# A graph network on one core: who gathers the rows of 782 steps, and how many of them are gathered ahead

## The reference

```python
# round 0
e = relu((x[dst] - x[src]) @ theta_w.T + theta_b + x[src] @ phi_w.T + phi_b)
x = layernorm(x + segment_max(e, dst))            # 0 where a node has no edge
# rounds 1 and 2
hv = x @ W_in + b_in
for W, b in ((W_u0, b_u0), (W_u1, b_u1)):
    m = relu(concat([hv[src], he]) @ W + b)       # he: 64 features of each edge
    hv = where(has_in, segment_max(m, dst) + hv, hv)
x = layernorm(x + relu(hv @ W_ro + b_ro))
```

## Time and profile before

| | |
|---|---|
| median of 3 runs | 4331.12 us (4325.9 to 4362.31) |
| span of the profiled execution, first to last instruction | 3216.1 us |
| time of the profiled execution | not given; the median is 1115.0 us over the span |
| busy: TensorE, GpSimd, VectorE, ScalarE | 2494.2, 2359.0, 1457.3, 196.1 us |
| mean granted TensorE clock | 0.922 |
| moved by DMA | 762.66 MB, mean 237 GB/s |
| gathers of steps: from x, from tables | 34, 2288 |
| row fetches of SyncE | 3072 |

### The profile page before, as it was taken

One profiled execution on the slowest core, in us unless ns is written; L12 is line 12 of the kernel. 1 busy time (PEld: TensorE's weight loads), 2 busy tenths in 40 slices (PEclk: granted clock), 3 DMA queues, 4 the chain that ended last, 5 costly groups with the idle time before them and its releaser, 6 DMA issues.

```text
span 3216.1 us, 33579 instructions
## 1 busy us (share of the span) xinstructions
PE 2494.2 (78%) x6386; PEld 1183.3 (37%) x6386; DVE 1457.3 (45%) x3424; ACT 196.1 (6%) x439; POOL 2359.0 (73%) x2484
## 2 busy tenths in 40 slices
PE   8776666666676888887887888688888888888877
PEld 6432222222223533333333333353333344333335
DVE  2675556555556533333433334323333343333337
ACT  2000000000002400000000000010000000000005
POOL 5777777777776677777777777667777777777765
PEclk9898888788877999999999999899999999999989
DMA  7666667666665777777777777687777777777764
GB/s 263 232 223 222 225 224 268 221 224 214 211 210 191 246 242 244 245 244 244 245 252 246 245 244 247 207 271 249 250 251 252 252 267 247 253 249 252 250 210 153
DMA packets 266593, 762.66 MB, mean 237 GB/s; under 512 B 57652, under 2 KB 113823, under 8 KB 229903
## 3 DMA queue, kind: packets, MB, share of 16 engines
q0 software_dynamic: 118896, 324.63, 33.2%
q1 hardware_dynamic: 94110, 356.95, 28.8%
q10 hardware_dynamic: 53376, 78.93, 7.9%
HBM read 413.88 MB, written 346.41 MB: 236 GB/s over the span
## 4 chain that ended last, share of the span: by engine, by line
POOL 39%; PE 17%; DMA 16%; issue 16%; SPq 7%; DVE 2%; ACT 2%; DVEq 0%; ACTq 0%; POOLq 0%
POOL gath L606 38%; DMA gath<-table,src_sb 14%; PE edge_ps L887 6%; SPq L530 4%; PE edge_ps L885 3%; PE edge_ps L778 3%; SPq L526 2%; PE side_ps L778 2%; PE edge_ps L864 2%; POOL gath L633 1%; DVE hist L410 1%; ACT x_sb L718 1%; DMA runs<-hist 1%; SPq L529 1%; DMA table<-hist 1%
## 5 line engine op out<-in xcount | busy, mean ns | idle before, releaser
L606 POOL DMA_INDIRECT gath<-table,src_sb x2288 | 2165.4, 946 | 745.0 <-issue 649.6
L410 DVE SCALAR_TENSOR_TENSOR hist<-hist,lift,edge_ps 128x256 f32<-128x256 f32 x2346 | 1127.0, 480 | 1564.3 <-PE edge_ps L887 1142.8
L887 PE MATMUL edge_ps<-gath,ident 128*128 128x512 f32 x1548 | 842.6, 627 | 328.0 <-DMA gath<-table,src_sb 326.4
L885 PE MATMUL edge_ps<-w_e,he_sb 128*128 128x512 f32 x1564 | 813.9, 602 | 5.5 <-DMA he_sb<-in_he 5.0
L864 PE MATMUL edge_ps<-gath,ident 128*128 128x512 f32 x740 | 476.3, 767 | 269.9 <-DMA gath<-table,src_sb 164.2
L887 PEld LDWEIGHTS edge_ps<-gath,ident 128*128 128x128 f32 x1548 | 275.7, 193 | 803.9 <-DMA gath<-table,src_sb 595.9
L885 PEld LDWEIGHTS edge_ps<-w_e,he_sb 128*128 128x128 f32 x1564 | 295.4, 194 | 352.7 <-issue 335.0
L864 PEld LDWEIGHTS edge_ps<-gath,ident 128*128 128x128 f32 x740 | 155.5, 236 | 532.5 <-DVE hist L410 317.1
L676 ACT COPY hv_sb<-side_ps 128x256 f32<-128x256 f32 x147 | 54.8, 373 | 2770.2 <-PE edge_ps L887 1842.9
L633 POOL DMA_INDIRECT gath<-runs,end_row x147 | 152.1, 1035 | 49.0 <-issue 43.6
L786 PE MATMUL edge_ps<-dst_f,onehot 128*128 128x512 f32 x200 | 78.0, 514 | 14.2 <-DVE onehot L333 14.2
(11 more groups left out here) (137 smaller groups left out, 1070.6 us busy)
## 6 DMA issues: line engine op xcount, KB each, us to landing
runs<-hist SPq DMA_DIRECT2D x285, 1024.0 KB, 5.0
he_sb<-in_he ACTq DMA_DIRECT2D x194, 256.0 KB, 2.9
late_sb<-table SPq DMA_DIRECT2D x3072, 1.0 KB
gath<-table,src_sb POOLq DMA_INDIRECT x2288, 3.4
table<-hist SPq DMA_DIRECT2D x72, 256.0 KB, 3.4
back_T<-x1T ACTq DMA_DIRECT2D x98, 128.0 KB, 3.2
runs<-hist SPq DMA_DIRECT2D x33, 256.0 KB, 2.9
x_sb<-in_x SPq DMA_DIRECT2D x49, 128.0 KB, 2.8
```

The source lines that it names most:

```text
L410: state = V.scalar_tensor_tensor(hist[:, s % H, :], hist[:, (s - 1) % H, :], lift[:, t:t + 1], edges, ALU.add, ALU.max)
L606: pool.indirect_dma_start(gath[:, s % G, :], None, a["x"] if s < RAW else tables[r], bass.IndirectOffsetOnAxis(src_sb[:, t:t + 1], 0)).the ...
L885: T.matmul(bank, he_sb[:, c % NHE, at:at + P], w_e[r - 1][:, :], start=True, stop=False)
L887: last = T.matmul(bank, ident[:, :], flat(edge_rows(s)), start=False, stop=True)
```

## The change

The two blocks of steps that SyncE fetched row by row go back to GpSimd, and all of `late_rows` goes, with its buffer `late_sb` (4 steps). The ring grows from 34 to 38 slots. Round 0's first 50 steps are gathered from x: 38 into the ring and 12 (`SPILL`) into tiles 32 to 43 of `x_sb`, which holds no features until later. `ring_place` leaves those 12 out of the ring's count, so step 50 takes the slot of step 0, step 88 that of step 50, and from there on a step waits for the step 38 before it. All 50 are raw for TensorE and ScalarE: 25 pairs are turned, copied and multiplied, where 17 were.

```diff
-G, H = 34, 24
+G, H = 38, 24
-RAW = G
-LATE_AT = (360, 720)
-LATE = 4
-LATE_ROWS = 16
+SPILL, SPILL_TILE = 12, 32
+RAW = G + SPILL
...
+        spill = x_sb[:, SPILL_TILE:SPILL_TILE + SPILL, :]
...
-        def by_pool(t):
-            return t < STEPS and late_group(t) is None
+        def real(t):
+            return t < STEPS
+
+        def in_spill(s):
+            return G <= s < RAW
+
+        def ring_place(s):
+            return s if s < G else s - SPILL
...
             def store_runs(r):
                 for c in range(CHUNKS):
-                    late_rows(r, c)
...
             def gather_edges(r):
-                for t in filter(by_pool, range(STEPS)):
+                for t in range(STEPS):
                     s = r * STRIDE + t
-                    if s % GS == 0 and s >= G:
-                        pool.wait_ge(group_summed, groups_to(s - G))
+                    if s % GS == 0 and s >= RAW:
+                        before = ring_place(s) - G
+                        pool.wait_ge(group_summed, groups_to(before if before < G else before + SPILL))
...
-                    pool.indirect_dma_start(gath[:, s % G, :], None, a["x"] if s < RAW else tables[r],
-                                            bass.IndirectOffsetOnAxis(src_sb[:, t:t + 1], 0)
-                                            ).then_inc(gathered[s % G // 2], 16)
+                    if in_spill(s):
+                        pool.indirect_dma_start(spill[:, s - G, :], None, a["x"],
+                                                bass.IndirectOffsetOnAxis(src_sb[:, t:t + 1], 0)
+                                                ).then_inc(spilled[(s - G) // 2], 16)
+                    else:
+                        pool.indirect_dma_start(gath[:, ring_place(s) % G, :], None, a["x"] if s < RAW else tables[r],
+                                                bass.IndirectOffsetOnAxis(src_sb[:, t:t + 1], 0)
+                                                ).then_inc(slot_filled(s), 16)
...
             def turn_raw(n):
-                pe.wait_ge(gathered[n], 2 * 16)
+                if in_spill(2 * n):
+                    pe.wait_ge(spilled[n - G // 2], 2 * 16)
+                else:
+                    pe.wait_ge(gathered[n], 2 * 16)
```

More of the change, by code:

```diff
@@ L37 @@
 XT_FIRST, XT_UNITS = 4, 3
-RAW = G
-LATE_AT = (360, 720)
-LATE = 4
-LATE_ROWS = 16
+SPILL, SPILL_TILE = 12, 32
+RAW = G + SPILL
 CONV, NEXT0, NEXT1, OUT = range(4)
-LATE_TURN = 3
-WEIGHTS_AT = (LATE_TURN + 1) * BODY
+EARLY_TURNS = 3
+WEIGHTS_AT = (EARLY_TURNS + 1) * BODY
 FIRST_X_CHUNK = 20
+assert SPILL % GS == 0 and SPILL_TILE + SPILL <= TILES
 assert TURNS == TILES and STRIDE % SC == 0 and H % SC == 0 and G % GS == 0 and STRIDE % HC == 0 and HC % GS == 0 and SC % GS == 0
@@ L174, in gnn_kernel @@
         raw_out = sem("raw_out")
+        spilled = [sem(f"spilled{q}") for q in range(SPILL // 2)]
         staged_written = [sem(f"staged_written{b}") for b in range(UNIT_BUFS)]
@@ L221, in groups_to, with slot_filled @@
             return s // STRIDE * GROUPS + min(s % STRIDE // GS + 1, GROUPS)
-        def late_group(t):
-            return next((n for n, first in enumerate(LATE_AT) if first <= t < first + LATE), None)
-        def by_pool(t):
-            return t < STEPS and late_group(t) is None
-        def pairs_in_slot(s):
-            return sum(by_pool(2 * q % STRIDE) for q in range(s // 2 % (G // 2), s // 2 + 1, G // 2))
+        def real(t):
[4 more added lines that the diff above has]
+            return s if s < G else s - SPILL
+        def pairs_in_slot(s):
+            at = ring_place(s) // 2
+            steps = [2 * q if 2 * q < G else 2 * q + SPILL for q in range(at % (G // 2), at + 1, G // 2)]
+            return sum(real(step % STRIDE) for step in steps)
+        def slot_filled(s):
+            return gathered[ring_place(s) % G // 2]
         def edge_rows(s):
[L233 to L236, removed]
+            if in_spill(s):
+                return spill[:, s - G:s - G + 2, :]
+            at = ring_place(s) % G
+            return gath[:, at:at + 2, :]
         def uses(n, u):
@@ L277, in back_tiles @@
         def back_tiles(r, i):
-            if r == 0 and i < 2 * (LATE_TURN + 2):
-                return range(max(0, 2 * (i - LATE_TURN - 2)), max(0, 2 * (i - LATE_TURN - 1)))
+            if r == 0 and i < 2 * (EARLY_TURNS + 2):
+                return range(max(0, 2 * (i - EARLY_TURNS - 2)), max(0, 2 * (i - EARLY_TURNS - 1)))
             return range(i, i + 1)
@@ L558, in write_out @@
                     sp.dma_start(a["out"][lo * P:NODES, :], outs(u)[0:left, 0, :]).then_inc(out_written[u % UNIT_BUFS], 16)
-            for n, first in enumerate(LATE_AT):
-                with nc.allow_non_contiguous_dma("small layouts"):
-                    sp.dma_start(late_src[n:n + 1, :].rearrange("o (p k) -> (o p) k", k=LATE), a["src"][:, first:first + LATE]
-                                 ).then_inc(late_listed, 16)
             for u in range(NU):
@@ L843, in wait_rows @@
             def wait_rows(s):
[L844 to L849 removed]
+                pe.wait_ge(slot_filled(s), 2 * 16 * pairs_in_slot(s))
             def first_rows():
@@ L870, in first_rows @@
                             back(t)
-                    if turn_no == LATE_TURN and at == BODY // 2 + GS:
+                    if turn_no == EARLY_TURNS and at == BODY // 2 + GS:
                         multiply_weights()
```

35 lines of the change are left out of this document (3 added, 32 removed).

## The result

The changed kernel took 3810.3 us, the median of 4 runs (3801.0 to 3815.8). The kernel before took 4346.7 us beside it (4 runs, 4325.9 to 4383.5). The ratio is 0.8785, with a 95% interval from 0.8735 to 0.8835: 12% less, where 0.9% more was forecast. The executions of this study ran on several chips. On two later ones the same pair stands at 3254.7 us against 3217.8, ratio 1.0115 (1.0100 to 1.0131), and at 3261.8 against 3226.3. I call the chips on which before takes 4334 us or more kind A (numbers 13 and 15, and the unnumbered chip of this result), and those on which it takes 3218 to 3226 us kind B (12 and 7). They differ in every kernel that ran on both. The runs come in series; within one series all kernels ran on one chip, and ratios are taken there only.

What follows compares the result with a forecast made beforehand. GpSimd's gathers, 1.25 us from start to start, were taken to set each round's end. 30.0 us for more gathers plus 8.8 at the start, added to 4331.1, gave 4369.9 us (+0.9%), range 4342 to 4393.

Steps and rivals of the forecast that it cites:

- part 1: GpSimd gathers 24 more steps over three rounds at 1.25 us each, +30.0 us; SyncE's dropped fetches are worth nothing.
- I take what lies around the span as unchanged: Outside the profiled span: the 1115.0 us between span and median time stay, so 38.8 us are added to 4331.1.
- signs of being wrong: TensorE sums step 68 before 158, the 1.25 us pace bends, a round's tail changes, or time minus span isn't 1115.
- Faster: Rival: SyncE's fetches cost time outside the span; if it went by number of instructions, 216 us, giving 4154; chance 0.07.
- rival of the stretched kernel: Rival: timed executions are the profiled one stretched by 1.347, so the change costs +52 us, giving 4383; chance 0.18.
- Sum: Whole kernel: 30.0 for the gathers plus 8.8 for the start gives +38.8 us, a span of 3254.9.
- Part 3: Round 0's start: TensorE's eight more raw pairs at 2.17 us make GpSimd wait 6.6 us at step 88, to 121.6.
- Part 4: ScalarE's weight loads queue behind raw copies; weight products come 12.3 us later, GpSimd is 8.8 us late from step 106.
- Part 2: Round 0's start: 16 more steps gathered from x in GpSimd's gap win 18.6 us, before TensorE's lag is counted.

Runs made afterwards that it cites:

- f3_half_dense: Kernel before with GpSimd gathering all steps and SyncE's fetches unused, but only half of them, batches of 16 in half as many chunks: 4063.2 us.
- f4_half_thin: Kernel before with GpSimd gathering all steps and SyncE's fetches unused, but only half of them, batches of 8 in as many chunks: 3827.0 us.
- h2_no_fetch_again: Kernel before without SyncE's fetches, GpSimd gathering all steps, ring of 34 and old start, on kind B: 3250.8 us, 1.0103 of before.
- h3_skip24: Kernel before with 24 steps neither fetched nor gathered, other rows summed in their place, on kind B: 3218.7 us, 1.0003 of before.
- h1_after_again: The changed kernel, nothing further altered, run again on kind B: 3254.7 us, 1.0115 of the kernel before.
- g1_incs_only: Kernel before without fetches, all steps gathered, plus 48 idle semaphore increments on SyncE in each of 192 chunks, on kind A: 3968.0 us, 0.915 of before.
- f1_static_rows: Kernel before with all steps gathered and SyncE's 3072 fetches unused, their row numbers written in the code, no register loads: 3816.1 us.
- f2_loads: Kernel before with all steps gathered and SyncE's fetches unused, all register loads kept but one fetch per batch of sixteen: 3784.9 us.

## Why the prediction was wrong

The step that failed is in part 1, on SyncE's 3072 fetches: their leaving "is worth nothing by itself: SyncE is on no chain that ends a round". On kind A, where the times were taken, the fetches are worth 628 us, 14% of the kernel, and SyncE is 40% of the chain. The premise was wrong in the profile of before, too: SyncE's queue has 7% of that chain, from 171.58 to 485.92. And the price of 0.23 us is a fetch's own duration; from one to the next it is 0.41, and with the load a batch fills nine tenths of a chunk. The forecast also took that one profile for the executions that had been timed. With it failed the line "I take what lies around the span as unchanged". On kind A the kernel before has a span of 4421.1 us in 4422.9, so the 1115 us lay inside the executions, in waits that the profile of before doesn't contain. Two of the prediction's own signs of being wrong came on kind A: the pace of 1.25 us bends, and the difference of time and span is not 1115.

The Trainium skill ("Runtime: NRT & Kernel Launch", "The ~15µs preamble/postamble breakdown") gives about 9 to 15 us for what lies around a kernel. The prediction weighed it and still left the 1115 us outside. The 2.0 us measured here between span and time are less than the page's figure, and 1115 was far more; the conclusion to draw was that profile and times were of unlike executions.

The rival *Faster* had the sign and the engine, but not the mechanism: it put the cost outside the span and by the number of instructions. It is inside, it does come with instructions, and it begins where SyncE's work of a chunk outlasts the chunk in the mean (f3_half_dense against f4_half_thin). The rival of the stretched kernel fell: the changed kernel on kind A is 1.171 times its time on kind B, the kernel before some 1.35 times.

On kind B, from which the profile came, the rest can be held against its steps.

- *Sum.* +38.8 us forecast, a span of 3254.9. Measured: span 3252.7, medians 3254.7 - 3217.8 = +36.9. That the sum is so near is in part luck: of its two terms one came out larger and the other less than half as large.
- *Part 1*, 24 gathers x 1.25 = +30.0. Measured +32.1 (h2_no_fetch_again against h3_skip24). There the fetches are indeed worth nothing. By the rule of the Trainium skill that the prediction quotes ("DMA: Bandwidth & Descriptors", "Issuing engines are not separate DMA queues") the 24 gathers would be near 0; the issue on GpSimd is the price, 32.1 us.
- *Part 3*, a wait of 6.6 us at step 88, to 121.6. Measured 8.30, to 122.22.
- *Part 4*, the last weight load issued at 126.1, the products at 136.1, waits of about 14 and 9 us, step 106 at 167.1. Measured: the last of the four loads of `w_e` issued at 127.0, the products at 137.18, waits of 13.66 and 7.57, step 106 at 167.02. VectorE did wait for the landing. Its timeline, and TensorE's behind it:

```profile
136.76 0.36 DVE L372 COPY x_sb<-b_in_col 128x128 f32<-128x128 f32 x2 [7.36 <-DMA w_e<-in_W_u]
```

```profile
137.18 3.72 PE L802 MATMUL edge_ps<-x_sb 128*128 128x256 f32 x8 [10.49 <-DVE x_sb L372]
...
162.06 2.98 PE L770 MATMUL edge_ps<-dst_f,onehot 128*128 128x512 f32 x4 [11.69 <-DVE onehot L338]
```

- *Part 2*, 18.6 us of head start that are lost again, and +8.8 in all. Against the profile of before, step 106 is 8.7 us later, as forecast. But in h2_no_fetch_again, with the old start, it stands at 161.09, so 5.9 us are the head start's, and the medians give +3.9 (h1_after_again against h2_no_fetch_again). On kind A it is 3810.3 against 3812.1 in different series. That the head start is lost is confirmed; the 8.8 was oversized.

On kind A the same waits stand at 11.18, 14.17 and 6.79 us, but they don't set the end: the mean pace of 1.25 us bends to 1.41 without any fetch on SyncE.

What stays open: what makes a chip one of kind A, and whether it is the chip at all and not the hour, its neighbours or the recording; four numbered chips were seen, one of them twice. In the traces of kind A the durations of gathers and of VectorE's steps are those of kind B (0.95 and 0.48 us), while the waits between the engines are longer, and TensorE's granted clock is 0.83 and not 0.91. SyncE's slow stretches explain the kernel before, but not the 546 us by which the changed kernel is longer there, since its SyncE has hardly an instruction: 35% of its chain is put down to releases that the trace doesn't hold, and that part is not explained. Nor is one execution of the kernel before beside g1_incs_only, which took 6626.1 us at a granted clock of 1.0.

## What to carry to other kernels

If the time of a run and the span of the profile differ by more than a few microseconds, they are not of the same execution: profile again before a forecast is built on either. An engine that only issues can be full, too; hold the length of its list for a stage against the stage's own length, from start to start and not by durations, and if it fills nine tenths, count what is queued behind it as exposed. Look for its queue in the chain as well: 7% stood there. Half of the fetches in batches of half the length cost 11 us where the same number in full batches cost over 200. And the loads that were brought forward on ScalarE cost it as much time as they took.

## What was not expected of the hardware

- On a chip of kind A SyncE came to take one semaphore increment of 17 ns in 0.7 or 1.4 us, in more than half of the batches: 48 of them lasted 14.1 us in the median. On a chip of kind B they lasted 2.8, and none of 1296 was longer than 17 ns.
- The kernel before took 4334 to 4420 us on some chips and 3218 to 3226 us on others, with equal durations of its gathers and of VectorE's steps; a ratio of two kernels was 0.88 on the one and 1.011 on the other.
- 3072 transfers of 1 KB in the queue of the stores cost at most some 31 us (f1_static_rows against f2_loads), with batches of 16 taking SyncE 10.0 us in the median, and over 12 in a quarter of the chunks of 11.3.
- A gather of 128 rows took 0.95 us, and 0.30 passed to the next where it waited for nothing, on both kinds of chip.
